# Cross-attention on one core: a new instruction order on every engine, and one softmax tile in eight finished by GpSimd

## The reference

```python
Q = (q @ Wq + bq)...; K = (k @ Wk + bk)...; V = (v @ Wv + bv)...     # q = x, k = v = the context
scores = jnp.einsum('bhqd,bhkd->bhqk', Q, K) / jnp.sqrt(jnp.float32(DH))
scores = scores * mask
attn = jax.nn.softmax(scores, axis=-1)
ctx = jnp.einsum('bhqk,bhkd->bhqd', attn, V).transpose(0, 2, 1, 3).reshape(b, s, H * DH)
x = q + ctx @ Wo + bo
return (x - mean) * rsqrt(var + LN_EPS) * gamma + beta
```

## Time and profile before

| | us |
|---|---|
| median of 3 runs | 3216.45 (3216.22 to 3218.16) |
| the profiled execution | 3215.79 |
| its span, first to last instruction | 3213.9 |
| PE busy | 2698.6 (84%) |
| DVE busy | 2139.6 (67%) |
| ACT busy | 1807.4 (56%) |
| POOL busy | 1157.6 (36%) |
| mean granted TensorE clock | 0.909 |

### The profile page before, as it was taken

One profiled execution on the slowest core, in us unless ns is written; L12 is line 12 of the kernel. 1 busy time (PEld: TensorE's weight loads), 2 busy tenths in 40 slices (PEclk: granted clock), 3 DMA queues, 4 the chain that ended last, 5 costly groups with the idle time before them and its releaser, 6 DMA issues.

```text
span 3213.9 us, 49972 instructions
## 1 busy us (share of the span) xinstructions
PE 2698.6 (84%) x14336; PEld 1834.1 (57%) x14336; DVE 2139.6 (67%) x4128; ACT 1807.4 (56%) x3809; POOL 1157.6 (36%) x1671
## 2 busy tenths in 40 slices
PE   6888888988888988888888878888788888888876
PEld 4555655555555655655555555555556555555554
DVE  5666666666666666666666766676666776667764
ACT  4655555555555555555565555555555555555553
POOL 2333333333333333333233434344333443434433
PEclk8989999999999999999999899898998988999888
DMA  5666556666556666656766565565655656556563
GB/s 154 131 149 152 123 125 145 155 146 154 126 122 152 148 150 151 129 120 154 183 160 126 129 139 136 124 150 125 141 134 133 148 130 140 134 127 148 128 138 92
DMA packets 1165324, 446.04 MB, mean 139 GB/s; under 512 B 1078880, under 2 KB 1078880, under 8 KB 1165280
## 3 DMA queue, kind: packets, MB, share of 16 engines
q1 hardware_dynamic: 1162160, 445.49, 62.1%
q10 hardware_dynamic: 3120, 0.01, 0.1%
HBM read 143.41 MB, written 33.55 MB: 55 GB/s over the span
## 4 chain that ended last, share of the span: by engine, by line
DVE 27%; PE 25%; ACT 19%; issue 16%; SPq 6%; DMA 4%; POOL 2%; DVEq 1%; ACTq 1%; POOLq 0%
DVE p L620 14%; ACT probs L463 11%; DVE score_ps L606 6%; PE fill_ps L297 5%; PE fill_ps L298 5%; PE fill_ps L299 5%; PE ctx_ps L365 4%; SPq L228 4%; DMA raw<-in_ct 4%; ACT p L475 4%; PE score_ps L343 2%; ACT q_hi L454 2%; PE score_ps L349 2%; PE score_ps L346 2%; DVE v_rest L643 1%
## 5 line engine op out<-in xcount | busy, mean ns | idle before, releaser
L463 ACT ACTIVATE probs<-score_ps,neg_max 128x512 f32<-128x512 f32 x1024 | 690.7, 685 | 886.9 <-POOL neg_max L804 886.9
L620 DVE SCALAR_TENSOR_TENSOR p<-probs,inv_sum,p 128x512 f16<-128x512 f32 x1024 | 946.1, 977 | 204.1 <-ACT p L475 204.1
L475 ACT ACTIVATE p<-probs,inv_sum 128x512 f16<-128x512 f32 x1024 | 655.9, 711 | 220.5 <-DVE inv_sum L614 220.5
L365 PE MATMUL ctx_ps<-pT,v 128*64 128x512 f16 x5120 | 611.9, 397 | 99.3 <-DVE ctx_lo L627 90.5
L606 DVE CUSTOM_DVE_ANT_0 score_ps<-score_ps,mask_sb 128x512 f32<-128x512 f32 x1024 | 676.7, 715 | 21.9 <-PE score_ps L349 20.9
L804 POOL TENSOR_SCALAR neg_max<-row_max 128x2 f32<-128x2 f32 x512 | 116.4, 227 | 1253.1 <-DVE row_max L606 1252.1
L365 PEld LDWEIGHTS ctx_ps<-pT,v 128*64 128x64 bf16 x5120 | 293.3, 114 | 403.7 <-issue 96.4
L343 PE MATMUL score_ps<-k_hi,q_hi 64*128 64x512 f32 x1024 | 305.6, 498 | 223.1 <-DVE k_lo L636 138.0
L297 PE MATMUL fill_ps<-xT_hi,wq_hi 128*128 128x512 f32 x512 | 245.1, 479 | 165.0 <-DVE v_rest L643 147.9
L343 PEld LDWEIGHTS score_ps<-k_hi,q_hi 64*128 64x128 f32 x1024 | 130.9, 204 | 366.7 <-issue 235.5
L636 DVE SCALAR_TENSOR_TENSOR q_lo<-fill_ps,bq_col,q_hi 128x512 fp32r<-128x512 f32 x128 | 95.9, 750 | 260.5 <-ACT q_hi L454 260.5
(11 more groups left out here) (60 smaller groups left out, 4551.5 us busy)
## 6 DMA issues: line engine op xcount, KB each, us to landing
raw<-in_xt SPq DMA_DIRECT2D x128, 256.0 KB, 3.3
raw<-in_ct SPq DMA_DIRECT2D x128, 256.0 KB, 3.6
mask_sb<-in_mask_Bx1xSxS_fk SPq DMA_DIRECT2D x128, 256.0 KB, 3.2
acc<-in_x SPq DMA_DIRECT2D x64, 256.0 KB, 3.4
partial<-acc SPq DMA_DIRECT2D x64, 256.0 KB, 2.6
acc<-partial SPq DMA_DIRECT2D x64, 256.0 KB, 3.3
out<-acc SPq DMA_DIRECT2D x64, 256.0 KB, 2.4
pT<-p SPq DMA_TRANSPOSE x512, 4.5
```

The lines of the kernel that those rows point to most:

```text
L365: mm = nc.tensor.matmul(ctx_ps[a * DH:(a + 1) * DH, :], v_piece[piece][:, t, col:col + DH], pT[:, par, :, a, plane, t, :], start=is_first, ...
L463: nc.scalar.activation(probs[:, i % 4, :], score_ps[:, i % 4, :], ACT.Exp, bias=neg_max[:, p % 2, i:i + 1], accum_out=row_sum[:, p % 2, i: ...
L475: nc.scalar.activation(p16[:, q, a, 0, :], probs[:, i % 4, :], ACT.Copy, scale=inv_sum[:, p % 2, i:i + 1]).then_inc(p_rounded, 1)
L620: nc.vector.scalar_tensor_tensor(out=p16[:, q, a, 1, :], in0=probs[:, i % 4, :], scalar=inv_sum[:, p % 2, i:i + 1], in1=p16[:, q, a, 0, :] ...
```

## The change

It has two parts.

First, one tile of every eight (tile 7 of each pair) gets its fp16 difference from GpSimd in two instructions; each engine's splits now count on a semaphore of their own, and whoever waited for `p_split` waits for the engine that owns the tile.

```diff
+E_TILES = 4
+POOL_TILES = (7,)
+VECTOR_TILES = tuple(i for i in range(TILES) if i not in POOL_TILES)
...
-FILL_BANK = dict(zip("O0 O1 K3 O2 O3 Q0 Q1 K0 K1 Q2 K2 V0 V1 V2 V3 Q3".split(),
+FILL_BANK = dict(zip("V2 V3 K3 O0 O1 O2 O3 Q0 K0 Q1 K1 Q2 K2 V0 Q3 V1".split(),
                      (0, 1, 2, 0, 1, 2, 0, 1, 2, 0, 1, 2, 0, 1, 2, 1)))
...
-        xc_split = sem("xc_split")
+        xc_split = {t: sem(f"{t}T_split") for t in "xc"}
...
-        p_split = sem("p_split")
+        p_split = {e: sem(f"p_split_{e}") for e in ("vector", "gpsimd")}
+        p_normalized = sem("p_normalized")
...
+        def split_done(n, p, i):
+            eng, tiles = ("gpsimd", POOL_TILES) if i in POOL_TILES else ("vector", VECTOR_TILES)
+            return p_split[eng], (n * PAIRS + p) * len(tiles) + tiles.index(i) + 1
...
+            def split_probs(at, p, tiles):
+                g, b, n = at
+                for i in tiles:
+                    q, a = i // 2, i % 2
+                    wait_alone(pool, p_rounded, tile_no(n, p, i))
+                    nc.gpsimd.tensor_scalar(probs[:, i % E_TILES, :], probs[:, i % E_TILES, :],
+                                            inv_sum[:, p % 2, i:i + 1], 1.0, ALU.mult, ALU.mult).then_inc(
+                        p_normalized, 1)
+                    sem_done, count = split_done(n, p, i)
+                    wait_alone(pool, p_normalized, count)
+                    nc.gpsimd.tensor_tensor(p16[:, q, a, 1, :], probs[:, i % E_TILES, :], p16[:, q, a, 0, :],
+                                            ALU.subtract).then_inc(sem_done, 1)
```

Second, every engine's program is one body with the step before (`prev`), the step itself (`here`) and the next (`nxt`), each left out at the ends, so that prologue and tail are the same list with parts missing. TensorE's:

```diff
+            def body(prev, here, nxt, out_weights, weights):
...
+                if here:
+                    fill(here, "V", 2)
+                    fill(here, "V", 3)
+                    scores(here, 2, range(0, 2))
+                    fill(here, "K", 3)
+                if prev:
+                    fill(prev, "O", 0)
+                if here:
+                    scores(here, 2, range(2, 3))
+                if prev:
+                    fill(prev, "O", 1)
+                if here:
+                    scores(here, 2, range(3, 4))
+                if prev:
+                    fill(prev, "O", 2)
+                if here:
+                    values(here, 0)
+                    scores(here, 3, range(0, 2))
+                if prev:
+                    fill(prev, "O", 3)
+                if nxt:
+                    fill(nxt, "Q", 0)
+                if here:
+                    values(here, 1)
+                    scores(here, 3, range(2, 4))
+                if nxt:
+                    fill(nxt, "K", 0)
+                    fill(nxt, "Q", 1)
+                    scores(nxt, 0, range(0, 1))
+                    fill(nxt, "K", 1)
+                    scores(nxt, 0, range(1, 2))
+                if here:
+                    values(here, 2)
+                if nxt:
+                    scores(nxt, 0, range(2, 4))
+                    fill(nxt, "Q", 2)
+                    fill(nxt, "K", 2)
+                    scores(nxt, 1, range(0, 1))
+                    fill(nxt, "V", 0)
+                    scores(nxt, 1, range(1, 2))
+                if here:
+                    values(here, 3)
+                if nxt:
+                    fill(nxt, "Q", 3)
+                    scores(nxt, 1, range(2, 4))
+                    fill(nxt, "V", 1)
```

More of the change, by code:

```diff
@@ L185, in _, with load_input @@
         def _(sp):
[L186 to L189, removed]
+            def load_input(at, t, tiles):
+                g, b, n = at
+                for i in tiles:
+                    if i == 0 and not (isinstance(n, int) and n == 0):
+                        if t == "x":
+                            wait_alone(sp, qk_ready["Q"], pair_no(n - 1, PAIRS - 1))
+                        else:
+                            wait_alone(sp, qk_ready["K"], pair_no(n - 1, PAIRS - 1))
+                            wait_alone(sp, v_ready, n * KT)
                     sp.dma_start(raw_input(t, i), (xt if t == "x" else ct)[b, i * P:(i + 1) * P, :]).then_inc(
@@ L287, in _, with load_mask, load_acc @@
-            prologue()
+            def load_mask(at, tiles):
+                g, b, n = at
+                for q in tiles:
+                    if not (isinstance(n, int) and n == 0):
+                        wait_alone(sp, masked, tile_no(n - 1, PAIRS - 1, 2 * q + 1))
+                    sp.dma_start(mask_sb[:, q, :], mask[b, 0, q * P:(q + 1) * P, :]).then_inc(mask_in[q], DMA)
+            def load_acc(at, tiles):
+                g, b, n = at
+                for q in tiles:
+                    if not (isinstance(n, int) and n == 0):
+                        wait_alone(sp, stored[q], n * DMA)
+                    sp.dma_start(acc[:, q, :], (x, partial)[g][b, q * P:(q + 1) * P, :]).then_inc(acc_in[q], DMA)
@@ L288, in _ @@
             batches(sp, body)
-            for q in range(QT):
-                store(1, LAST, B - 1, q)
             for q in range(QT):
@@ L301, in _, with fill @@
             users = {}
-            def fill(n, kind, k):
+            def fill(at, kind, k):
+                g, b, n = at
                 bank_no = FILL_BANK[f"{kind}{k}"]
@@ L432, in _ @@
             batches(pe, body)
-            for q in range(QT):
-                fill(LAST, "O", q)
         @block.scalar
@@ L589, in _ @@
+            for n, vec in (("q", bq), ("k", bk), ("v", bv)):
+                with nc.allow_non_contiguous_dma(reason="once, 1024 values to columns"):
+                    act.dma_start(bias_col[n][:, :], vec.rearrange("(j p) -> p j", p=P)).then_inc(bias_in, DMA)
+            for dst, vec in ((bo_b, bo), (gamma_b, gamma), (beta_b, beta)):
+                act.dma_start(dst[:, :], vec.partition_broadcast(P)).then_inc(rows_in, DMA)
             batches(act, body)
-            for q in range(QT):
-                standardize(LAST, q)
```

987 lines of the change are left out of this document (511 added, 476 removed).

## The result

The changed kernel takes 2563.93 us, median of 4 runs (2561.32 to 2566.25), against 3216.34 for the kernel before on the same chip: a ratio of 0.797, with a 95% interval of 0.796 to 0.799. The profiled execution took 2565.99.

The account below looks back on a forecast made before the run. TensorE bounds by resource, losing 18 us of 96 a period to order. Head 88 + 15 x 79.5 + (80 + 7) + 15 x 80.5 + tail 72.5 = 2647.5, plus 1.9 around the span: 2649, taken as 2650; range 2570 to 2810.

Parts of the forecast that it names:

- Step 1: TensorE's floor a period: 77.5 us without stops or low clock, plus 0.5 for more block changes, 78.0.
- Step 5: Remaining TensorE waits from contended splits at three tight places: 1.5 us a period in the first pass, 2.5 in the second.
- step 3: Tile 7 moved to GpSimd: VectorE loses 3.7 us a period, gets 1.5 of contention; GpSimd gains 8; buys slack for margins.
- step 2: Hand layout of the new engine lists: every margin positive, 0.6 to 4 us, and three old TensorE waits gone.
- The three old waits: TensorE's waits behind VectorE for V bank, K and context remainders, each once a period; claimed gone by construction.
- Step 4: Queues: negated maxima behind GpSimd's tile 0 to 2 us late a period, counted in waits; transpositions cost 0; DMA 0.77 busy.
- Step 6: Ends and switch: first fill near 20 us, head 88, change of weights 7 on an 80 period, tail 72.5.
- Rival A: VectorE and in-order queues bound, GpSimd two-input instructions slowing splits: period 82 to 88, 2712 to 2898 us; chance 0.25.
- rival B: Waits move through ScalarE's strict order, one or two low-clock stops a period stay: period 88 to 97, 2898 to 3177; 0.08.
- Rival C: GpSimd's split holds negated maxima four times a period, scores stop, clock falls: period 98.5, 3223 us; chance 0.03, other causes included.
- Rival D: TensorE's weight loads, not its matmul pace, are its only limit, so VectorE would bound: 2185 us; chance 0.01.

Follow-up runs that it names:

- e4: The changed kernel with VectorE's remainder of V1 moved ahead of one split and one mask: 2569.56 us, ratio 0.799.
- e1: The changed kernel without the moved tile, so VectorE splits tile 7 right behind tile 6: 2546.29 us, ratio 0.791.
- e6: e1 with 8 unused VectorE statistics instructions a period added, 5 us: 2548.84 us, ratio 0.792.
- e5: e1 with the four x tiles loaded right behind the q weights at the start, and ScalarE rounding q weights first: 2538.45 us, ratio 0.789.
- e2: The kernel before (old order) with tile 7's difference on GpSimd, behind the pair's scaled sums: 3319.99 us, ratio 1.032.
- e8: e1 with 16 unused VectorE statistics instructions a period added, 10 us: 2576.88 us, ratio 0.801.
- e3: The changed kernel with the next batch's K0 remainder and first four masks put back behind VectorE's splits: 2768.60 us, ratio 0.861.

## Why the prediction was right, and where it was wrong

TensorE's old waits went as forecast, and the measured time still lies 6 us below the range: steps 1 and 5 were both too high, and step 3 had the sign of the tile wrong.

The spans add up as 89.0 + 82.96 + 1076.6 + 84.7 + 1162.65 + 68.3 = 2564.2, against the 2647.5 of the sum: 83.3 us too many. **Step 1** (the floor) put a TensorE that never stops at 78.0 us a period; it is 76.90. The subtraction had 0.6 too many, the 0.5 for more block changes came on top: 1.1 x 30 = 33 us. What a subtraction of waits and slow stretches leaves in is the restart. In the timeline above the matmul after the 0.22 us wait begins 0.61 behind the one before it and the next 0.33 behind that, where 0.23 is the pace: 0.48 lost for 0.22 waited, and 0.6 by the periods. That this is the 0.6 of the subtraction is argued, not shown. The block lengths that step 2 used give another floor, 16 x 2.84 + 16 x 0.8 + 4 x 4.43 = 76.0, which is 0.9 too low: the truth lay between the two.

**Step 5** failed, and is the larger part. It gave 1.5 and 2.5 us of residual waits a period, because contended splits would be late at three tight places. In the first pass there are none, but for the first period (6.1 us over the rest); in the second there is one, at V3, worth 0.6. That is 16.4 + 28.4 = 45 us. A late split was the right mechanism for the one wait there is; three places and a microsecond at each were not. The term had no row behind it: step 2 had already found every margin positive, and step 5 paid for them again. The range carried the mistake on, as its low end was a period of 77.5 with everything else as forecast, and two such terms were high in the same direction. A floor that is "nothing idle" has no error upwards by waits, and the low end must lie under it.

**Step 2** stood. The three old waits went, as laid out. The tightest places were the right ones: V3 for V1's bank lost 0.22 us in the second pass, and `e4` found the next, pair 2's query 1. The hand layout had V1's at 1.4 of margin, so it was off by up to 1.6 where splits are slowed by GpSimd.

**Step 3** had the sizes and not the sign. VectorE was to be freed of 2.2 us (3.7 less 1.5 of contention); `e1` against the full change gives 1.9 in the first pass and 1.4 in the second. GpSimd was to gain 8 and gained 7.9, though its pair costs 2.29 us and not 2.0. But "what the tile really buys is slack for the margins" is refuted by `e1`, 17 us faster without it, and by `e6`, where 5 us more load on VectorE cost nothing. It also took "nothing is lost on TensorE" for granted: GpSimd's difference holds a `probs` buffer, an exponential comes 0.5 us late for it, and with it the sums and GpSimd's product, which then slows a split at the tightest place. Step 4 had looked at the negated maxima behind the tile and found 0 to 2 us, but not at this buffer. The rule that was weighed there (the Trainium skill, GPSIMD Engine Reference, Engine selection: VectorE for elementwise work on a tile, GpSimd about twice as slow with two inputs) pointed the right way. The trace has 1.22 against 0.75 (a split with GpSimd idle) for the difference itself, 1.6 times, and 2.29 against 0.75 for the tile, since GpSimd needs two instructions for what VectorE does in one.

**Step 4** held for the queues: TensorE waits for no transposition, which lands in 4.4 us (4.5 before), and the DMA engines are 0.80 to 0.81 busy where 0.77 was worked out for a longer period.

**Step 6**: head 89.0 (88 forecast), switch 84.7 (87), tail 68.3 (72.5). The head is right by errors that cancel. The first fill came at 23.46, so 13.3 us later than before and not 10. Behind it TensorE is idle 9.5 us (89.0 - 56.0 - 23.5) where it was 19.3, so the interleaving took 9.8 and not 13.5. And TensorE's own work took 56.0 us and not 62.0, at a granted clock of 0.92 against 0.85, which the sum didn't have. `e5` starts its first fill 12 us earlier and keeps 9.3 of them.

Of what would show it, these came out: TensorE's idle time, its clock between the head and the tail but for the first period (0.92) and the switch (0.96), no remainder's wait above 20 us, VectorE's longest waits for scores (280.6 us), and the splits near 1.0 (810.9 us for 896, so 0.91). VectorE at 58.6 and 62.5 a period is under the 62 to 67, and the GpSimd pair is over 2.0. Rival A needed some 80 us a period of VectorE. Of rival B's stops with the low clock there is none in either pass: the granted clock is 1.00 in both windows. Rival C's mechanism, a GpSimd tile ahead of the negated maxima, is what `e2` ran into in the old order; in the new one GpSimd waits 0.6 us for the tile's input, not 3.8. Rival D: the Trainium skill (Perfetto Trace Analysis, Identifying the Most-Contended Engine) judges TensorE's headroom by its share of peak work and by the load of weights. In the period without any idle time that load is 52.24 us of 76.90, so 68%; read alone it would promise headroom, and an order that takes waits away has none left to find. The share of peak work was not looked at.

## What to carry to other kernels

In a kernel whose first engine is idle by waits that come once a period, lay its floor in two ways, by subtraction (77.5 here) and by adding up uninterrupted blocks (76.0), and let the range reach under the lower one: this order came to a period with no idle time at all, at 76.90. Before moving work to relieve an engine, put load on that engine and look whether the time rises; here 5 us a period did not make it rise, so 1.9 us of relief had little to bring. And look at what the moved work will hold on its new engine: a late input delays what stands behind it in the queue (3.8 us at each tile in `e2`), and a buffer that it keeps longer delays whoever writes it next (0.51 us at one exponential, and with it 0.6 a period).

## What the runs showed of the hardware

**Contention between VectorE and GpSimd goes both ways, but not alike.** A split has two operands in SBUF and takes 0.75 us with GpSimd idle (at 1111.67 in the kernel after). With two-input GpSimd instructions beside it for over 90% of its time it took 1.20 to 1.83 us (44 splits of the kernel after). How much depends on which instruction falls on it where: beside the same product and sum it is 1.83 in the one timeline above and 1.23 in the other. With one-input instructions (the tile's scaling, negated maxima) beside it for over 90% of its time it took 0.74 (80 splits), so nothing.

Those one-input instructions mostly pay themselves. A pair of negated maxima, two elements a row, takes 0.64 us beside the split at 2087.99 and 0.19 at 2090.02, beside a remainder that reads PSUM; over the kernel after it is 0.55 on average for the 302 that meet a split and 0.19 for the other 210. Their mean is 405 ns there and 227 in the old order with the tile, where 63 of 512 meet one. The tile's scaling takes 0.70 in `e2`, where splits run beside it for 0.2 us at most; in the new order 95 of 128 take about 1.2, each with splits beside it for over 0.6 us, and 33 still 0.70. VectorE's work on a PSUM operand stays within 0.67 to 0.75. The Trainium skill (SBUF — State Buffer, Who interferes with whom) says that a VectorE instruction with two SBUF inputs contends with a GpSimd instruction that reads SBUF; these rows agree and put sizes to it. Spans on GpSimd are rough, so the second half rests on counts and means.

**A very short wait of TensorE costs more than its own length.** A gap of 0.11 us (`e4`) and one of 0.22 (the kernel after) once a period both made the period 0.6 longer, one of 0.44 (`e8`) 0.8. Part of it is how a gap is counted: matmuls here start 0.23 apart and last 0.39, so a gap of 0.22 means a start that comes 0.38 late, and the next one is late by 0.10 more.

**A stop of 4.39 us at a granted clock of 1.00 was followed by 2.9 us of loss** at the 1.2 GHz level (`e3`), like the stops of the old order.
